# Last pass of a fused decoder layer on one core: odd experts' sums added by accumulating transfers into SBUF in place of GpSimd's additions, every block's rows kept by ScalarE, and the last block normalised in two halves

## What is computed

```python
def ffn(hidden_states, ...):                     # 4096 tokens of 256 numbers, 8 experts, 2 chosen for each token
    x = hidden_states.reshape(-1, H)
    scores = softmax(x @ gate_w.T)
    topk_w, topk_idx = top_k(scores, 2)
    topk_w = topk_w / (topk_w.sum(-1, keepdims=True) + 1e-20)
    # an expert takes at most 1280 tokens, in the order of the tokens
    comb = zeros((N, E)).at[arange(N)[:, None], topk_idx].add(topk_w * keep)
    g, u = einsum('nh,eih->nei', x, we_gate), einsum('nh,eih->nei', x, we_up)
    eo = einsum('nei,ehi->neh', silu(g) * u, we_down)
    y = einsum('neh,ne->nh', eo, comb)
    sh = silu(x @ ws_gate.T) * (x @ ws_up.T) @ ws_down.T        # the shared experts
    return (y + sh).reshape(orig_shape)

x = layernorm(x + ffn(x))
```

## Time and profile before

| what | us |
|---|---|
| median of 3 runs | 1419.07 (1417.61 to 1420.23) |
| the profiled execution, its own time | 1418.96 |
| its span, from the first to the last instruction | 1417.2 |
| PE, DVE, ACT, POOL busy in it | 1311.9, 1088.3, 923.1, 467.0 |
| granted clock of TensorE, mean | 0.969 |

### The profile page before, as it was taken

The page is one execution under the profiler, slowest core; times in us unless marked ns, Lnnn a source line. Parts: engine busy times, 40 slices in busy tenths (PEclk is TensorE's granted clock), DMA queues, the critical chain, the costliest instruction groups (busy, mean ns, idle before and its releaser), DMA issues. The chain is left out here.

```text
span 1417.2 us, 27263 instructions
## 1 busy us (share of the span) xinstructions
PE 1311.9 (93%) x8312; PEld 778.1 (55%) x8312; DVE 1088.3 (77%) x2228; ACT 923.1 (65%) x1771; POOL 467.0 (33%) x484
## 2 busy tenths in 40 slices
PE   3999999999999999999999999999578999999984
PEld 2434454444444444444444444444356799999964
DVE  5889889889978988987898888897377745555475
ACT  3387767777677777777777677777356555656444
POOL 3334203301501420240151011021146636666663
PEclk9699999999999999999999999999899999999997
DMA  5454435344334324434442442350245457687752
GB/s 174 128 162 130 137 114 150 96 136 133 121 108 141 121 79 143 120 114 123 136 141 81 153 129 77 108 148 2 84 151 190 154 146 141 132 168 132 151 180 89
DMA packets 109945, 181.47 MB, mean 128 GB/s; under 512 B 20352, under 2 KB 67584, under 8 KB 105728
## 3 DMA queue, kind: packets, MB, share of 16 engines
q1 hardware_dynamic: 94656, 159.90, 36.8%
q0 software_dynamic: 14592, 19.41, 7.7%
q10 hardware_dynamic: 576, 0.79, 0.3%
HBM read 99.67 MB, written 79.30 MB: 126 GB/s over the span
## 5 line engine op out<-in xcount | busy, mean ns | idle before, releaser
L790 ACT ACTIVATE prob<-ps_sc 128x512 f32<-128x512 f32 x1024 | 551.5, 601 | 194.9 <-PE ps_sc L1050 194.1
L833 DVE TENSOR_REDUCE nm<-ps_ring 128x1 f32<-128x512 f32 x1024 | 638.4, 679 | 50.9 <-PE ps_ring L1035 50.2
L1035 PE MATMUL ps_ring<-qk 48*128 48x512 f32 x1024 | 406.5, 469 | 13.9 <-DMA qk<-hbm_self 7.1
L1050 PE MATMUL ps_sc<-qk 50*128 50x512 f32 x1024 | 388.6, 453 | 11.0 <-ACT prob L790 10.0
L1050 PEld LDWEIGHTS ps_sc<-qk 50*128 50x128 f32 x1024 | 161.1, 186 | 301.3 <-ACT prob L790 218.2
L1067 PE MATMUL ps_out<-prob,va 128*32 128x512 f32 x2048 | 275.0, 609 | 1.6 <-ACT ot L669 0.7
L1831 PE MATMUL ps_gu<-x2f,we 128*128 128x256 f32 (+1 forms) x1344 | 225.8, 323 | 3.9 <-ACT sg L1492 2.4
L1831 PEld LDWEIGHTS ps_gu<-x2f,we 128*128 128x128 f32 x1344 | 190.9, 193 | 20.5 <-DVE h L1722 3.1
L1035 PEld LDWEIGHTS ps_ring<-qk 48*128 48x128 f32 x1024 | 166.1, 188 | 44.1 <-DVE nm L833 26.2
L1831 PE MATMUL ps_dn<-we,hf 128*128 128x256 f32 x864 | 112.8, 282 | 10.2 <-DVE totals L1805 10.2
L598 POOL TENSOR_TENSOR rstd<-mv,eps 128x2 f32<-128x2 f32 x32 | 6.3, 197 | 344.8 <-DVE mv L921 344.8
(11 more groups left out here) (171 smaller groups left out, 1586.6 us busy)
## 6 DMA issues: line engine op xcount, KB each, us to landing
qk<-hbm_cross SPq DMA_DIRECT2D x384, 64.0 KB, 2.3
qk<-hbm_self SPq DMA_DIRECT2D x372, 64.0 KB, 2.3
hbm_self<-stage SPq DMA_DIRECT2D x16, 1024.0 KB, 3.9
hbm_cross<-stage SPq DMA_DIRECT2D x16, 1024.0 KB, 4.1
slots_x<-zeros SPq DMA_DIRECT2D x8, 1360.0 KB, 5.9
xs<-slots_x SPq DMA_DIRECT2D x40, 272.0 KB, 3.4
weraw<-w_moe SPq DMA_DIRECT2D x11, 768.0 KB, 4.4
x2in<-x SPq DMA_DIRECT2D x16, 512.0 KB, 4.3
```

The costliest lines, as they stand in the source:

```text
L790: nc.scalar.activation(prob[:, s % 2, j, :], ps_sc[:, score_bank(h.cur, HG * s + j), :], ACT.Exp, scale=HD ** -0.5).then_inc(exp_done[a], 1)
L833: nc.vector.tensor_reduce(nm[:, g % 2, r:r + 1], bank(slot), axis=AX.X, op=ALU.max, negate=True).then_inc(max_done[a], 1)
L1035: nc.tensor.matmul(bank(slot), qk[rows, 0, pair, P * c:P * c + P], qk[rows, 1, pair, :], start=True, stop=True).then_inc(smax_done[a], 1)
L1050: nc.tensor.matmul(ps_sc[:, score_bank(inst, n), :], qk[rows, 1, h // 2, P * c:P * c + P], qk[rows, 0, h // 2, :], start=True, stop=True). ...
```

## The change

The change takes POOL's eight additions (L1443) and SP's eight loads of the odd sums (L1364) out. In their place POOL starts eight accumulating transfers, which read the odd sum of block n from `x2` in DRAM and add it to `total(n)` in SBUF. They stand in POOL's list one behind the other ahead of the first block's scale and shift, behind a wait for all of the experts' rows, and behind waits for the even sums. DVE adds the kept rows of blocks n = 0 and 1 already in the slots (10, 0) and (10, 1) (`add_kept`), ahead of their accumulating transfers; for later blocks it waits for the transfer and adds in the block's own slot, both pairs one behind the other. ACT now keeps the rows of every job up to 14 in `ym`, so PE's `down` waits for ACT's copy in every job, and only the last block is read from `ps_dn` by DVE. The last block goes through DVE, POOL, ACT and SP in two halves of two tiles.

```diff
         @block.sync
-            def load_odd(n):
-                sp.dma_start(xin[:, n % HELD, :, 0:D], odd_rows[JOBS[B + n][0]]).then_inc(x_in[n % HELD], 16)
...
-            for n in range(HELD):
-                load_odd(n)
             for n in range(6, B):
                 load_even(n)
 
-            for n in range(B):
-                if n + HELD < B:
-                    sp.wait_ge(both_done, n + 1)
-                    load_odd(n + HELD)
-                if n >= 2:
-                    sp.wait_ge(norm_done, TT * (n - 1))
-                    sp.dma_start(out[JOBS[B + n - 2][0], :, :, :], total(n - 2)).then_inc(out_done, 16)
-            for n in range(B - 2, B):
+            for n in range(B - 1):
                 sp.wait_ge(norm_done, TT * (n + 1))
                 sp.dma_start(out[JOBS[B + n][0], :, :, :], total(n)).then_inc(out_done, 16)
-            sp.wait_ge(out_done, 16 * B)
+            for pair in range(2):
+                at = slice(2 * pair, 2 * pair + 2)
+                sp.wait_ge(norm_done, TT * (B - 1) + 2 * pair + 2)
+                sp.dma_start(out[JOBS[2 * B - 1][0], :, at, :], total(B - 1)[:, at, :]).then_inc(out_done, 16)
         @block.gpsimd
-            def both(n):
+            for c in range(NCH):
+                pool.wait_ge(added[c], 16 * CT * NE)
+            for n in range(B):
                 pool.wait_ge(even_in[n // 3], 16 * (2 if n // 3 == 2 else 3))
-                pool.wait_ge(x_in[n % HELD], in_of_odd(n))
-                nc.gpsimd.tensor_tensor(total(n), total(n), xin[:, n % HELD, :, 0:D], ALU.add).then_inc(both_done, 1)
+                if n < EARLY:
+                    pool.wait_ge(total_done, 2 * n + 2)
+                nc.gpsimd.dma_start(total(n), odd_rows[JOBS[B + n][0]], accum_op=ALU.add) \
+                    .then_inc(scattered[n] if n < 3 else added[n - 3], 16)
...
+            for pair in range(2):
+                q, at = (B - 1) % 2, slice(2 * pair, 2 * pair + 2)
...
+                nc.gpsimd.tensor_tensor(rstd[:, q, at, :], mv[:, q, at, 1:2], eps[:, at, :], ALU.add).then_inc(last_done, 1)
...
         @block.scalar
             def keep(j):
                 for pair in range(2):
                     act.wait_ge(dn_done, of_job(j, pair))
+                    if j >= B + MARGIN:
+                        act.wait_ge(total_done, 2 * (j - MARGIN - B) + pair + 1)
...
-                    if c == 1 and LATE < j <= B + MARGIN:
+                    if c == 1 and LATE < j:
                         keep(j - 1)
...
         @block.vector
+            def add_kept(n):
+
+                if n < EARLY:
+                    dve.wait_ge(even_in[n // 3], 48)
+                else:
+                    sum_in(dve, n)
+                for pair in range(2):
+                    mine = total(n)[:, 2 * pair:2 * pair + 2, :]
+                    dve.wait_ge(ym_done, out_of_job(B + n, pair))
+                    nc.vector.tensor_tensor(mine, mine, ym[:, (B + n) % MARGIN, 2 * pair:2 * pair + 2, :],
+                                            ALU.add).then_inc(total_done, 1)
...
             for j in range(LATE, NJ):
                 for c in range(IC):
                     product(j, c)
                     h_lo(j, c)
+                    if j == LATE:
+                        add_kept(c)
                     if (j, c) in MOMENTS_AT:
                         moments(MOMENTS_AT[j, c])
-            moments(B - 1)
+            last_moments()
         @block.tensor
                 if j == LATE:
                     pe.wait_ge(ym_done, out_of_chunk(CHUNKS - 2 + pair, CT - 1))
-                elif j > B + MARGIN:
-                    pe.wait_ge(total_done, 2 * (j - 1 - B) + pair + 1)
                 elif j:
                     pe.wait_ge(ym_done, out_of_job(j - 1, pair))
```

More of the change, by code:

```diff
@@ L1289, in out_of_chunk, with sum_in @@
             return 2 * LATE + CT * g + t + 1
-        def in_of_odd(n):
-            return 16 * (len(range(n % HELD, B, HELD)) + n // HELD + 1)
+        def sum_in(eng, n):
+            if n < 3:
+                eng.wait_ge(scattered[n], PER_BLOCK * len(range(n, B, HELD)) + 16)
+            else:
+                eng.wait_ge(added[n - 3], 16 * CT * NE + 16)
         def split_next(kk, j):
@@ L1610, in _ @@
                         norm(NORM_AT[j, c])
-            for n in range(6, B):
-                norm(n)
+            norm(B - 2)
+            for t in range(TT):
+                if t % 2 == 0:
+                    act.wait_ge(last_done, 2 * t + 4)
+                nc.scalar.activation(total(B - 1)[:, t, :], total(B - 1)[:, t, :], ACT.Identity, scale=rstd[:, (B - 1) % 2, t, :],
+                                     bias=shift[:, (B - 1) % 2, t, :]).then_inc(norm_done, 1)
         @block.vector
@@ L1791, in _, with stats @@
             by_pairs(dve, CHUNKS, chunk, NCH)
+            def add_kept(n):
+                if n < EARLY:
+                    dve.wait_ge(even_in[n // 3], 48)
+                else:
+                    sum_in(dve, n)
[4 more added lines that the diff above has]
+                                            ALU.add).then_inc(total_done, 1)
+            def stats(n, t):
+                nc.vector.bn_stats(st6[:, n % 2, t, :], total(n)[:, t, :]).then_inc(moments_done, 1)
             def moments(n):
                 q = n % 2
[L1795 to L1808 removed]
+                if n < EARLY:
+                    sum_in(dve, n)
+                else:
+                    add_kept(n)
+                for t in range(TT):
+                    if n >= EARLY and t % 2 == 0:
+                        dve.wait_ge(total_done, 2 * n + t // 2 + 1)
+                    stats(n, t)
                 if n >= 2:
@@ L1813, in moments, with last_moments @@
                     nc.vector.bn_aggr(mv[:, q, t, :], st6[:, q, t, :]).then_inc(moments_done, 1)
+            def last_moments():
+                n, q = B - 1, (B - 1) % 2
+                sum_in(dve, n)
+                dve.wait_ge(norm_done, TT * (n - 1))
+                for pair in range(2):
+                    at = slice(2 * pair, 2 * pair + 2)
+                    mine = total(n)[:, at, :].rearrange("p t d -> p (t d)")
+                    dve.wait_ge(dn_done, of_job(B + n, pair))
+                    nc.vector.tensor_tensor(mine, ps_dn[:, pair, :], mine, ALU.add).then_inc(total_done, 1)
+                    dve.wait_ge(total_done, 2 * n + pair + 1)
+                    for t in (2 * pair, 2 * pair + 1):
+                        stats(n, t)
+                    for t in range(2):
+                        dve.wait_ge(moments_done, 2 * TT * n + 4 * pair + 1 + t)
+                        nc.vector.bn_aggr(mv[:, q, 2 * pair + t, :], st6[:, q, 2 * pair + t, :]).then_inc(moments_done, 1)
             for j in range(LATE, NJ):
```

26 lines of the change are left out of this document (11 added, 15 removed).

## The result

The change makes the kernel faster. The changed kernel took 1409.76 us as the median of 8 runs (1404.0 to 1413.33), the kernel before 1419.65 (1417.61 to 1427.05, 8 runs): a ratio of 0.9916 with a 95% interval of 0.9893 to 0.9939. The forecast was 1428.5, so its sign was wrong. What came is the first rival, short issues, put at 1408.5 us with a chance of 0.33.

The account below looks back on a forecast made before the run. DVE's chain of slots was taken to bound the pass, with POOL's issues deciding: 1397.9 + 8 x 3.6 = 1426.7 us of span, 1428.5 us of time, some 9.5 us slower; range 1407.5 to 1440 us.

Parts of the forecast that it names:

- the first rival: POOL's issuing of the eight adding transfers is short and does not grow with rows: faster, 1408.5 us, chance 0.33.
- What is X?: Step pricing POOL's issue of one 512-row adding transfer from indirect transfers' rows: 3.6 us, middle of 2.28 and 4.97.
- X: Time POOL needs to issue one adding transfer of 512 rows, without the 0.3 us gap; taken as 3.6 us.
- lower reading, 2.28: POOL's issue time if only the added pass grows with rows: 4 x 0.571 = 2.28 us.
- "none" and "all": Bounds of POOL's issue time: 0.976 us if none of it goes with the rows, 6.19 us if all does.
- The point, if POOL issues for long: Product(13, 0) waits for eight issues, then 4.8 us of scale and shift, norm, silu and hand-overs; end 1397.9 + 8 X.
- the threshold of 1.1: Issue time in us from which POOL's eight issues set the end later than 1406.7 us.
- The point itself, if POOL is free in time: Product(13, 0) starts at 1363.3 us, behind ACT's norm of block 0 and silu; the end is 1406.7 us.
- Do the transfers keep up?: Adding transfers take 4.3 us each, first landing about 1356.6 us against need at 1355.7; within 1 us or hidden.
- What the change takes off: From product(13, 0) to the end: 47.5 us less 2.8 for slowed additions and 1.3 in the last block, 43.4 us.
- Two slowed additions at 1.38 us each: DVE's additions in slots (13, 0) and (13, 1), slowed beside POOL's, go from 2.05 to 0.67 us; 2.8 us saved.
- The interval's miss of more than 2 us: Sign of error: product(13, 0) to the end off 43.4 us by over 2 means something besides POOL's reads slows DVE.

Follow-up runs that it names:

- the run of 32: The changed kernel with each block's accumulating transfer issued as four of 128 rows, 32 issues in place of 8: 1436.07 us, ratio 1.0038 to the kernel before.

## Why the prediction was wrong

**"What is X?" is the step that failed.** It read 0.571 us out of two indirect rows as the price of one pass over 128 rows, and set X at 3.6 us, 3.9 with the gap. Measured is 1.31 us with any gap in it. In the sum that is the whole way from 1426.7 us to 1406.7, the forecast's end if POOL is free in time. Rows do cost, but 0.14 us for 128; the fixed part of 0.75 us, which the step had at 0.405, carries more than half. The direct form adds for 0.13 us where the indirect rows differ by 0.571, so that difference belongs mostly to the indirect form. The step took its lower reading, 2.28, from the same difference, so no reading between "none" and "all" was free of it. The Trainium skill's rule ("DMA: Bandwidth & Descriptors", the section on the GpSimd path), many descriptors before the cost shows, is nearer to the measurement than my reading of the rows: rows of 1 KB add 0.56 us to a transfer of 512 rows. The whole issue, 1.31 us, lies above the plain indirect row's 0.976 us, where that rule would have left it.

**"The point, if POOL issues for long" holds.** With 28.47 us of issues the shift, the norm, the silu and the product followed as written, in 4.4 us for 4.8. The margin was narrow: eight issues ended 0.77 us ahead of the moments. In the forecast's terms X is 1.31 - 0.3 = 1.0 us, just below the threshold of 1.1. The threshold was nearly right: the cover left in the trace, 0.77 + 0.64 = 1.4 us for all eight issues, puts it at about 1.2.

**"The point itself, if POOL is free in time".** Product(13, 0) came at 1364.81 in place of 1363.3 us. The pass began 0.45 us later, and DVE waited 1.18 us for the first landing, which by "Do the transfers keep up?" was to be hidden or within 1 us and was put at nothing here: foretold within a microsecond ("first lands at about 1356.6", needed at 1355.7; DVE began at 1357.45).

**"What the change takes off" was too small.** It gave 43.4 us from product(13, 0) to the end; it took 1405.5 - 1364.8 = 40.7. Three terms make up the 2.7. Slots (13, 0) to (15, 1) other than (14, 1) were to keep 5.70 us and took 5.46, 1.2 us in all: both additions and then four statistics in a row take less than the two in turns. Slot (14, 1) took 4.80 for 5.25, as I added whole durations of ACT's pieces whose rows overlap their successors'. The last block gained 2.35 for 1.3: ACT's part gained the 1.0 us forecast, POOL's 0.45 for 0.3, and I had left out that the store behind the last norm is half as long (from that norm's end 2.4 us, where it was 3.25). DVE's aggregates of the second half are 0.30 us in place of 0.83, but DVE's part as a whole gained only 0.1, as it waits 0.29 us for PE between the halves. That the rival's 1408.5 us lies so near the measured 1409.76 is in part luck: product(13, 0) came 1.5 us late, and the rest was 2.7 us shorter.

**"Two slowed additions at 1.38 us each"** was right in kind and size: without POOL's reads no addition was slow. The interval's miss of more than 2 us is thus not the one that the forecast named, of DVE being slowed by something else. **"Do the transfers keep up?"** was right in its verdict and pessimistic in its size: 2.7 us a transfer for 4.3.

The gain, then: 7.4 us from POOL's reads being out of DVE's way (measured alone), 2.4 from the halves (measured alone), and some 2 to 2.5 from the early additions of blocks 0 and 1, the order of additions and statistics, and the keeping. Of these only the keeping was measured alone (at most 0.5). The rest of this part is arithmetic on slots, not shown by a run.

## What to carry to other kernels

Before pricing a queue's issues by rows of another form, run one transfer of the new form and one of a quarter of its size; the two give a fixed part and a part by rows, and here the whole forecast hung on them. Anything that an engine issues or waits for ahead of a small instruction is a wait of all behind that instruction: count the microseconds of cover (here 0.77 to the moments) rather than whether there is any. A GpSimd instruction that reads SBUF holds up VectorE's operations with both inputs in SBUF, so give such work to transfers, let it only write, or feed VectorE one input from PSUM; and fill an engine's short waits with independent work, which brought some 6 us more here.

## What was new of the hardware

- A direct adding transfer that POOL starts costs it 0.89 us with 128 rows of 1 KB, 1.31 with 512, and 1.5 to 1.6 with 1024; a plain one of 512 rows 0.79. The durations shown for single issues overlap, up to 7 us in the run of 32.
- Adding into SBUF moved 197 GB/s by itself, and SP's plain loads 338 to 420 GB/s at the same place before the change (1350 to 1357 us). An adding transfer of 512 KB counts 528 packets, a plain one that POOL starts 144.
- A DVE operation with both inputs in SBUF that begins beside a reading POOL instruction ends about 0.55 us behind it (additions of 2.05 to 2.90 us for 0.68); one already under way, one with an input in PSUM, and one beside a POOL write of 2.4 us keep their 0.67 to 0.69 us.
- PE's 24 down products take 2.99 us or, late in the pass, up to 5.4. Behind waits of 4.6 us and more they took 4.4 to 5.4 us in every trace that has such a wait (5.27 behind 7.17, 4.42 behind 7.16 in another trace of the same kernel, 5.12 behind 4.62); behind waits of 2.4 to 3.1 us they took 3.0 to 3.1 us but for two cases (4.60 behind 2.64, 4.57 behind 2.65). In the changed kernel the granted clock is 0.54 in the 5.27 us of its last down products, so near the lower of its two levels (1.2 and 2.4 GHz), and 1.00 in the 2.99 us of the job before; in the kernel before it is 0.53 in the 5.30 us of the earlier trace rows.
